# Local attention in a decoder block: who divides the first pair of heads by its sums, ACT or GpSimd

## The reference

```python
def _layer(x, wqkv, qs, ksc, wo, lg, lb, w1, b1, w2, b2):
    h = shift_token(x)
    q, k, v = jnp.split(h @ wqkv, 3, axis=-1)          # 8 heads of 64
    q = l2norm(q) * qs
    k = l2norm(k) * ksc
    q, k = rotary_xpos(q, k)
    o = local_attention(q, k, v)                       # windows of 128
    x = x + o @ wo
    ...
def local_attention(q, k, v):
    ...
    sim = jnp.einsum('bhwid,bhwjd->bhwij', bq, bk)     # 128 queries, 256 keys
    sim = jnp.where(mask, -jnp.finfo(sim.dtype).max, sim)
    attn = jax.nn.softmax(sim, axis=-1)
    out = jnp.einsum('bhwij,bhwjd->bhwid', attn, bv)
```

## Time and profile before

| | |
|---|---|
| median of 3 runs | 2064.73 us (2061.18 to 2072.19) |
| profiled execution, its own time | 2069.69 us |
| its span, first to last instruction | 2067.9 us |
| TensorE busy in the span | 1955.6 us (95%) |
| VectorE | 1646.7 us (80%) |
| ACT | 1536.3 us (74%) |
| GpSimd | 1247.1 us (60%) |
| mean granted TensorE clock | 0.975 |

### The profile page before, as it was taken

The page is one execution under the profiler, slowest core; times in us unless marked ns, Lnnn a source line. Parts: engine busy times, 40 slices in busy tenths (PEclk is TensorE's granted clock), DMA queues, the critical chain, the costliest instruction groups (busy, mean ns, idle before and its releaser), DMA issues. The chain is left out here.

```text
span 2067.9 us, 55494 instructions
## 1 busy us (share of the span) xinstructions
PE 1955.6 (95%) x19772; PEld 1414.9 (68%) x19772; DVE 1646.7 (80%) x3925; ACT 1536.3 (74%) x3610; POOL 1247.1 (60%) x1184
## 2 busy tenths in 40 slices
PE   5999999999999999869999998999789999999997
PEld 4445555455555554348888887888678888887887
DVE  7888888888888889459999995665379999985775
ACT  2688888888888888628999987454279998985443
POOL 3445566544445443667888775554368887765775
PEclk9999999999999999979999999999889999999999
DMA  4233333333333334301000001200100000001211
GB/s 139 84 112 117 117 107 117 122 117 117 118 118 129 129 131 138 113 32 56 13 2 3 2 13 30 69 16 1 44 2 8 8 3 3 17 8 47 74 49 46
DMA packets 90759, 132.90 MB, mean 64 GB/s; under 512 B 13888, under 2 KB 41280, under 8 KB 90496
## 3 DMA queue, kind: packets, MB, share of 16 engines
q1 hardware_dynamic: 87936, 120.97, 18.0%
q0 software_dynamic: 2560, 8.39, 1.1%
HBM read 47.14 MB, written 29.89 MB: 37 GB/s over the span
## 5 line engine op out<-in xcount | busy, mean ns | idle before, releaser
L1208 DVE TENSOR_REDUCE MX<-PS 128x1 f32<-128x512 f32 x1024 | 642.3, 683 | 96.6 <-PE PS L683 93.3
L1019 ACT ACTIVATE PT<-PS 128x512 f32<-128x512 f32 x1024 | 552.2, 614 | 93.0 <-PE PS L698 90.4
L698 PE MATMUL PS<-QS,KS 64*128 64x512 f32 x1024 | 365.9, 436 | 6.8 <-ACT PT L1019 5.0
L683 PE MATMUL PS<-KS,QS 64*128 64x512 f32 x1024 | 349.4, 432 | 6.6 <-DMA KS<-HL 2.4
L698 PEld LDWEIGHTS PS<-QS,KS 64*128 64x128 f32 x1024 | 164.2, 185 | 251.6 <-issue 216.1
L714 PE MATMUL PS<-PT,VP 128*17 128x512 f32 x2048 | 270.3, 600 | 3.8 <-ACT OT L1026 2.9
L1587 POOL TENSOR_TENSOR PB<-PB,RC 128x512 f32<-128x512 f32 (+1 forms) x192 | 182.1, 957 | 136.6 <-DVE RC L1337 136.6
L790 PE MATMUL PS<-WQ,XT 64*128 64x512 f32 x1536 | 225.1, 428 | 20.6 <-DVE RB L1291 7.4
L1083 ACT ACTIVATE PB<-PB,NMf 128x256 f32<-128x256 f32 (+1 forms) x512 | 242.0, 490 | 0.0
L1327 DVE CUSTOM_DVE_ANT_0 PB<-PS,mk,RN 128x256 f32<-128x256 f32 (+1 forms) x512 | 203.9, 445 | 2.4 <-PE PS L861 1.6
L683 PEld LDWEIGHTS PS<-KS,QS 64*128 64x128 f32 x1024 | 167.8, 186 | 50.1 <-issue 37.3
(11 more groups left out here) (196 smaller groups left out, 4628.6 us busy)
## 6 DMA issues: line engine op xcount, KB each, us to landing
od<-OT SPq DMA_DIRECT2D x64, 256.0 KB, 2.8
QS<-HL SPq DMA_DIRECT2D x96, 128.0 KB
KS<-HL SPq DMA_DIRECT2D x96, 128.0 KB
QS<-HL SPq DMA_DIRECT2D x48, 256.0 KB
KS<-HL SPq DMA_DIRECT2D x48, 256.0 KB
OC<-od SPq DMA_DIRECT2D x32, 256.0 KB
OC<-rs SPq DMA_DIRECT2D x32, 256.0 KB
X<-x SPq DMA_DIRECT2D x8, 512.0 KB, 4.7
```

The costliest lines, as they stand in the source:

```text
L683: pe.matmul(PS[:, bank, :], QS[rows, s, h // 2, qt * P:(qt + 1) * P], KS[rows, s, h // 2, :], start=True, stop=True).then_inc(fills("amax" ...
L698: pe.matmul(PS[:, bank, :], KS[rows, s, pair, kt * P:(kt + 1) * P], QS[rows, s, pair, :], start=True, stop=True).then_inc(fills("score", v ...
L1019: act.activation(PT[:, kt % 2, 2 * i + half], PS[:, TURNS["score", vb, g, kt, half, i][0], :], ACT.Exp).then_inc(drains("score", vb, g, kt ...
L1208: dve.tensor_reduce(MX[:, vb % 2, h // 8, qt, c:c + 1], PS[:, TURNS["amax", vb, h, qt][0], :], AX, ALU.max).then_inc(drains("amax", vb, h, ...
```

## The change

`SCALED_BY_ACT` becomes empty. ACT no longer has anything to do in `wscale`, and GpSimd multiplies all four pairs. The functions themselves stay as they are; the count that the semaphore of GpSimd's scalings has to reach follows from `scaled`.

```diff
-SCALED_BY_ACT = (0,)
+SCALED_BY_ACT = ()
```

## The result

The changed kernel takes 2160.87 us (median of 4 runs, 2160.09 to 2163.44) against 2065.72 us (4 runs, 2061.18 to 2072.19). The ratio is 1.0459 (95% interval 1.0438 to 1.048): 4.6% slower. The span of the profiled execution is 2158.3 us, 90.4 more than before, and the mean granted clock 0.966 against 0.975.

A forecast was written before the change was run, and what follows sets the result against it. TensorE, busy 98.99 of 100 us, was taken as the bound; 84 us for a ring through GpSimd's wait plus 15 for the clock, 99, on a 2064.73 median, less up to 3 for ACT, gave 2160 us, range 2125 to 2200.

The forecast's parts named there:

- ACT's gain: ACT loses two activations in each of 64 turns, 54.2 us; costed at nothing, up to 3 us at layer ends.
- a ring of one turn: First four heads' reciprocal, GpSimd's multiply, clamp to L1579, TensorE's L844, next such reciprocal: about 12.35 us a turn.
- The pieces: Reciprocal to multiply 0.08, multiply to clamp 1.00, clamp to L1579's end 4.38, to L844 0.10, then L844 to next reciprocal.
- The last piece: From L844's start to the end of the next first-four-heads reciprocal: 7.00, 7.43, 6.65, 6.65 us in four turns.
- part-only rival: VectorE's stretch from L844 to the reciprocal shrinks to 6.5 us every turn: +60, 2125 us without a clock fall; chance 0.10.
- 84 us for the ring: Four turns of the reciprocal-to-reciprocal chain lengthen by 5.6 us on average; 15 such fours in two layers give +84.
- 15 us for the clock: TensorE's wait before L844 lowers the granted clock in half of the turns, 0.5 us each: +15, ends 0 and 54.
- Sum, 99 and 2160: 84 plus 15 is 99: 2168.7 on the profiled execution, 2164 on the median, rounded to 2160 with ACT's relief.
- The shared port: VectorE's L1302 beside a GpSimd multiply takes 1.47 against 0.69 us; added multiply costed at nothing, 48 if meeting each turn.
- hidden: Rival: GpSimd's 20% free time and TensorE's up to 2.21 us of room cover the wait; 2065 us; chance 0.05.
- faster: Rival: ACT, relieved of 0.9 us a turn, gives some 10 us at the layers' ends; 2055 us; chance 0.03.
- The clock in nearly each turn: Rival: TensorE's clock falls nearly every turn, or the port adds: 84 + 30 to 54, about 2195 us; chance 0.15.

The follow-up runs named there:

- the first experiment: Against the changed kernel, pair 0's multiply moved a turn later in GpSimd's queue, ahead of pair 1 and behind L1579: 2070.44 us, ratio 1.0019 to the kernel before.
- The last experiment: The changed kernel plus one more GpSimd multiply ahead of the clamp, on an unread buffer, in 28 of 32 turns a layer: 2218.76 us, ratio 1.0733.

## Why the prediction was right, point by point

- *TensorE is the bound before, and what counts is whether it starts to wait*: right. It went from 98.99 to 88.57 of 100 us; the forecast had 86.
- *ACT's gain is nothing*: right. With pair 0 a turn later ACT has the same relief, and the time is by its ratio 4 us above that of the kernel before, not below. The 3 us that the sum took off for ACT are not seen.
- *The wait stands ahead of the clamp and closes a ring of one turn*: right, shown from both sides. The wait alone costs 29 us (31 expected), the multiply alone 18 (20 expected), and taking pair 0 out of the ring gives all but 4 us back.
- *The pieces*: 0.08, 1.00, 4.38 and 0.10 came out within 0.01. The last piece, 7.00, 7.43, 6.65, 6.65 in the four turns, came out 8.15 (1156.44 to 1164.59), 7.33, 6.55 and 6.59. The first of these holds a fall of the clock (below), the rest are 0.06 to 0.10 shorter: the part-only rival had the right sign and almost no size.
- *84 us for the ring*: the four turns took 50.47, and without the turn of 13.71 the other three took 36.76 against 36.98 in the sum, 0.07 less each; over 60 turns that makes the ring about 80.
- *15 us for the clock, a fall in half of the turns at 0.5*: near in sum, wrong in both factors. The clock fell 13 times in the sixty turns, against twice in the kernel before. Six falls lie in the first and last turns of the layers, where I can't price them. The other seven made turns of 13.5 to 13.7 us, where turns in the same place of the four took 12.1 without a fall: some 10 us together. So falls were rarer and dearer than the term had them. Ring and clock then give about 90 (an estimate), and 89.5 was measured in the sixty turns.
- *Sum, 99 and 2160*: the cost of the change was 90.4 us between the profiled executions, 9 less than the 99. That 2160 met 2160.87 within 1 us is in part luck: the 9 us too many were made up for by a base 5 us lower, by up to 3 for ACT and by rounding.
- *The shared port costs nothing more*: right for the added multiply, which starts behind L1302 in the turns shown. What the prediction did not see is that an old encounter of L1302 with another multiply, hidden before, now costs time: see below.
- *L844 waits for L1579, 80 to 100 us in all, 60 times*: right. The matmuls of L844 waited 63.4 us in 44 times for L1579, and another 16.1 us in 14 times that the profile puts down to "issue", as at 1170.17. There too L844 starts 0.10 us behind L1579's end, as it does in 58 of the sixty turns, so these waits are for L1579 as well. Together they are 79.5 us, at the lower end of what was said.

Of the rivals, *hidden* is refuted by the sixty turns, *faster* by the first experiment, *part only* by its last piece, which is 0.06 to 0.10 shorter where it needed 0.15 to 0.9. *The clock in nearly each turn* falls with the 13 falls in sixty turns. The last experiment had 36, and beyond the ring's 50 it lost only some 7 us more than the changed kernel.

## What to carry to other kernels

Before a piece of work is moved to an engine with a low busy share, look at what is queued behind its new place, and at when its input arrives there. Its wait then belongs to everything behind it, also to work for other tiles that had nothing to do with it. If that work leads round through other queues to the very input that is waited for, and the sum of the ring's pieces is more than the busiest engine's work, that sum is the time of a turn, however idle each engine looks; the cure is another place in the queue (here one turn later, 95 us to 4), not less work.

## What the runs showed that I had not expected

The first of the four turns after shows two things at once. All rows are of the changed kernel. Busy time and granted clock in 1155 to 1160 and, for later, in two other stretches:

```profile
1155.00:1160.00 5.00, 3.50 (x40) 3.28 (x42) 2.92 (x11) 1.75 (x5) 3.79 (x5) 0.71 0.00 0
1207.00:1212.00 5.00, 4.94 (x58) 4.41 (x60) 2.48 (x7) 2.41 (x5) 4.04 (x4) 0.66 0.02 3
1256.00:1261.00 5.00, 3.74 (x62) 3.39 (x64) 3.77 (x13) 3.08 (x9) 3.98 (x4) 1.00 0.35 105
```

Then TensorE's timeline, with what lies between these rows left out, and VectorE's addition a turn earlier:

```profile
1157.52 3.40 PE L891 MATMUL PS<-PTB,V 128*64 128x128 f32 x32
1183.55 1.97 PE L891 MATMUL PS<-PTB,V 128*64 128x128 f32 x32
1206.91 0.99 PE L844 MATMUL PS<-ident,RA 64*128 64x64 f32 x16 [1.47 <-POOL RA L1579]
1257.20 0.99 PE L844 MATMUL PS<-ident,RA 64*128 64x64 f32 x16 [1.46 <-POOL RA L1579]
...
1148.51 1.47 DVE L1302 TENSOR_TENSOR RA<-RA,RB 128x512 f32<-128x512 f32 x1
```

The clock fell behind the wait of 2.15 us at 1156.44 and did not fall behind those of 1.28 and 1.31; the 32 matmuls of L891 took 3.40 us there and take 1.97 at full speed. And the wait was 2.15 and not 1.3 because in the turn before VectorE's addition L1302, beginning beside a multiply on GpSimd (1148.39), had taken 1.47 in place of 0.69, as in the earlier trace rows. Before, TensorE's own work hid such an addition: L844 started 10.78 us apart over the one of the earlier trace rows (1118.80 and 1129.58), no more than the 11.00 of the turn from 1151.98 to 1162.98. Now it lies in the ring and lengthens TensorE's wait, and the longer wait is followed by half speed. Four of the seven falls priced above came in this way, behind waits of 2.15 to 2.18.

The other three came without such an addition, behind waits of 1.46 or 1.47, as the one at 1206.91 (granted clock 0.66 in 1207 to 1212). Behind the like wait of 1.46 at 1257.20 the clock stayed at full speed (1.00 in 1256 to 1261). So the length of the wait alone does not say whether the clock falls, and these rows don't show what else decides. The Trainium skill ("TensorE: Matmul & The Clock Gate", Part 1) warns of pauses that let the clock fall; the trace agrees in so far as each of the 13 falls in the sixty turns comes with a wait before L844. The last experiment adds that more frequent falls (0.90 of full speed in 1100 to 1200) need not cost much.
